# Scaling the softmax rows on GpSimd in place of VectorE, in an attention block between two LoRA mixture layers

## The chip, the cores and the metric

The program runs on one core of a Trainium2 chip. The metric is the time of one execution on the device, in microseconds (us). Lower is better. Its engines are named as the profile names them: PE is TensorE's matmul, PEld its weight load, DVE is VectorE, ACT is ScalarE, POOL is GpSimd, SP is SyncE, which issues most of the transfers.

## The reference

The input x has 4 sequences of 256 tokens with 512 features. It goes through three layers, each added to it: half a dense layer with 8 LoRA experts of which two are chosen for each token, an attention layer, and the first layer again. The attention is what the change touches:

```
q = (x @ wq)  32 heads of 128;  k, v = x @ wk, x @ wv  8 heads of 128
q, k = rope(q), rope(k)
scores = q k^T * 128**-0.5, allowed where j <= i and j > i - 128
attn = softmax(scores)
x = x + (attn @ v) @ wo
```

With sequences of 256 and a window of 128, a block of 128 queries has allowed keys only in its own block (at or before its diagonal) and in the block before it (past its diagonal).

## The kernel before

Every matmul of float32 data is done as three matmuls of rounded parts (hi\*hi, hi\*lo, lo\*hi). So each operand is split: ACT writes the rounded part `hi`, and DVE or POOL subtracts it from the source to get `lo`. DVE does it where the source is in PSUM, POOL where it is in SBUF.

The attention is a loop over 8 groups, one for each head of k and v. A group g has two halves (`hf` 0 and 1, two sequences each), and a half has 8 slots `s`: two sequences times four query heads. The unit of softmax work is numbered u = 16 g + 8 hf + s. The groups 1 to 6 are one loop body; groups 0 and 7 are written out apart. Each engine runs its own instruction stream in the fixed order of its own `group` function, and semaphores tie the streams together. In one slot:

- PE computes a ninth part of the projections of q, k and v for the next half (`project`, L1102, 9 matmuls), then the scores of unit u+1 (`scores`, L1121 to L1124), then the two transposes of the probabilities of unit u-1 (`p_transpose`, L1132). In slots 1 and 5 it goes on with probabilities times v for the sequence before (`values`, L1145), in slots 2, 3, 6 and 7 with the product with wo (`out_project`, L1160), which in slots 3 and 7 waits for the sum that DVE adds to x in the same slot (`x_add`, L841).
- DVE runs `softmax_norm` of unit u (the inverse of the row sums, L819, and two multiplications of prob, 128x128 each, L822), then `rope_sum` (L787) and `rope_cos` (L778), then the lower part of the transposed probabilities of u-1 (`p_lo`, L828), then `softmax_min` of unit u+1 (L806 to L814). Where a slot has them, `x_add` comes first and `o_lo` (L834) last.
- ACT computes the exponentials of unit u (`softmax_exp`, L550), splits weights, copies the half-swapped projection for rope (`rope_swap`, L523), and writes the upper part of the transposed probabilities of u-1 (`p_hi`, L558).
- POOL multiplies the swapped copy by the sines (`rope_sin`, L368), masks the transposed probabilities of u-1 (`p_part`, L375), computes the lower part of q or k (`rope_lo`, L385), and then the lower parts of the next weights (`weights`, L360). These stand at fixed slots: four of wo in slot 4 of half 0, one of wk in slot 5, two of wq in slot 7 and two in slot 0 of half 1, one of wv in slot 2 of half 1.

In half 1 of group 7 nothing more is projected. DVE's `ffn_start` begins the last layer there, and POOL runs `norm_rstd(2, ...)` in slots 1 and 5: 14 small dependent operations (L238 to L249) and a memset, between the slot's other work and its `p_part`.

The probabilities of a unit lie in `prob[:, s % 2, 0:2*P]`, those of the next unit in the other half of the buffer. The semaphore `norm_done` tells PE that a unit is scaled.

```
wait(pe, ptlo_done, u)        # in p_transpose(u, s), behind pe.wait_ge(norm_done, u + 1)
```

Of the kernel before, what the change touches and what calls it, by code (L numbers as in the profile page):

```python
# [24 lines left out]
P = 128  # L25
# [50 lines left out]
def macaron(nc, x_in, wq, wk, wv, wo, w_base, b_base, w_router, lora_a, lora_b, ident_in, mask_in, side_in, rope_in, out):  # L76
    ctx = ExitStack()
    with ctx:
        def sb(name, shape, dt=F32):
            return ctx.enter_context(nc.sbuf_tensor(name, shape, dt))  # L80

        def sem(name):
            return ctx.enter_context(nc.semaphore(name))
# [24 lines left out]
        prob = sb("prob", [P, 2, 3 * P])  # L108
# [8 lines left out]
        rinv = sb("rinv", [P, 2, 2])  # L117
# [73 lines left out]
        part_done = sem("part_scores_done")  # L191
        s_done, min_done, exp_done = sem("scores_done"), sem("min_done"), sem("exp_done")
        rinv_done, norm_done = sem("rinv_done"), sem("norm_done")
        parted, mask_turn = sem("pT_parted"), sem("mask_turn")
        t_done, pthi_done, ptlo_done = sem("pT_done"), sem("pT_hi"), sem("pT_lo")
        pv_done, othi_done, otlo_done = sem("pv_done"), sem("oT_hi"), sem("oT_lo")
        c_done, x_added = sem("wo_done"), sem("attn_x_done")
# [11 lines left out]
        def wk_pos(g):  # L209
            return 10 * g  # L210

        def wq_pos(g, i):
            return 10 * g + 1 + i

        def wv_pos(g):
            return 10 * g + 5

        def wo_pos(g, i):
            return 10 * g + 6 + i
# [106 lines left out]
        @block.gpsimd  # L326
        def _(pool):
            nc.gpsimd.memset(ones, 1.0).then_inc(preset, 1)
            nc.gpsimd.memset(ebuf[:, :, :, :], -1.0).then_inc(preset, 1)
            nc.gpsimd.memset(two[:, :, :], -1.0).then_inc(preset, 1)  # L330
            zero = nc.gpsimd.to_reg(0.0)

            def bias(f, t):

                if f == 0 and t == 0:
                    pool.wait_ge(prep_hi, 8)
                pool.wait_ge(xn_done, NT * 2 * f + t + 1)
                nc.gpsimd.tensor_tensor(x[:, t, :], x[:, t, :], half_bias[:, :], ALU.add).then_inc(biased, 1)

            steps = [0]  # L340

            def then(ins):

                steps[0] += 1
                ins.then_inc(pool_step, 1)
                pool.wait_ge(pool_step, steps[0])

            def norm_rstd(ln, t0, t1):

                pool.wait_ge(aggr, NT * ln + t1)  # L350
                rstd_steps(nc.gpsimd, then, t0, t1)
                nc.gpsimd.memset(gate_pool[:, :], 0.0).then_inc(rstd_done, 1)

            def split_lo(n, slot, hi, lo):

                pool.wait_ge(conv_hi, n + 1)
                src = raw[:, slot, :]
                if len(hi.shape) == 3:
                    src = src.rearrange("p (t n) -> p t n", t=KT)
                nc.gpsimd.tensor_tensor(lo, src, hi.bitcast(F32), ALU.subtract).then_inc(conv_lo, 1)  # L360

            def rope_sin(j, m):

                r = 5 * j + m
                w = swap[:, m % 2, :].rearrange("p (b s) -> p b s", b=2)
                tab = rope[:, 1 if m == 0 else 3, :].unsqueeze(1).broadcast_to([P, 2, SEQ])
                pool.wait_ge(swap_done, r + 1)
                nc.gpsimd.tensor_tensor(w, w, tab, ALU.mult).then_inc(t2_done, 1)  # L368

            def p_part(u, s):  # L370

                pool.wait_ge(ptlo_done, u + 1)
                pool.sem_inc(mask_turn, 1)
                h = s % G
                nc.gpsimd.affine_select(pT_both[:, :, 2, h, :], pT_both[:, :, 1, h, :].bitcast(F32),  # L375
                                        pattern=[[0, 2], [1, P]], compare_op=ALU.is_ge, fill=zero,
                                        base=0, channel_multiplier=-1).then_inc(parted, 1)

            def rope_lo(j, m, par):

                r = 5 * j + m
                hi = k[0][:, par, :] if m == 0 else q[0][:, par, m - 1, :]
                lo = k[1][:, par, :] if m == 0 else q[1][:, par, m - 1, :]
                pool.wait_ge(qhi_done, r + 1)
                nc.gpsimd.tensor_tensor(lo, rot[:, m % 2, :], hi.bitcast(F32), ALU.subtract).then_inc(qlo_done, 1)  # L385

            def weights(g, hf, s, last):
                if hf == 0 and s == 4:
                    for i in range(G):
                        split_lo(wo_pos(g, i), (6 + i) % RING, wo_s[0][:, i, :], wo_s[1][:, i, :])  # L390
                if hf == 0 and s == 5 and not last:
                    split_lo(wk_pos(g + 1), (6 + 4) % RING, wk_s[0][:, :, :], wk_s[1][:, :, :])
                if (hf, s) in ((0, 7), (1, 0)) and not last:
                    for i in ((0, 1) if hf == 0 else (2, 3)):
                        split_lo(wq_pos(g + 1, i), (6 + 5 + i) % RING, wq_s[0][:, i, :], wq_s[1][:, i, :])
                if hf == 1 and s == 2 and not last:
                    split_lo(wv_pos(g + 1), (6 + 9) % RING, wv_s[0][:, :, :], wv_s[1][:, :, :])

            def group(g, first, last):
                for hf in range(2):  # L400
                    for s in range(SLOTS):
                        split, m = (ENDS.get(c) if not (last and hf == 1) else None for c in (s - 1, s))
                        if m is not None and m < 5:
                            rope_sin(2 * g + hf + 1, m)
                        if last and hf == 1 and s in (1, 5):
                            norm_rstd(2, s // 2, s // 2 + 2)
                        if not (first and hf == 0 and s == 0):
                            p_part(16 * g + 8 * hf + s - 1, s - 1)
                        if split is not None and split < 5:
                            rope_lo(2 * g + hf + 1, split, 1 - hf)  # L410
                        weights(g, hf, s, last)

            for t in range(NT // 2):
                bias(0, t)
            norm_rstd(0, 4, NT)
            split_lo(0, 0, wk_s[0][:, :, :], wk_s[1][:, :, :])
            for i in range(KT):
                split_lo(1 + i, (1 + i) % RING, wq_s[0][:, i, :], wq_s[1][:, i, :])
            for t in range(NT // 2, NT):
                bias(0, t)  # L420
            norm_rstd(1, 0, 2)
            norm_rstd(1, 2, 4)
            split_lo(5, 0, wv_s[0][:, :, :], wv_s[1][:, :, :])
            for m in range(6):
                if m < 5:
                    rope_sin(0, m)
                if m:
                    rope_lo(0, m - 1, 0)
            group(0, True, False)
            with pool.Fori(1, KV - 1) as g:  # L430
                group(g, False, False)
            group(KV - 1, False, True)
            p_part(16 * KV - 1, SLOTS - 1)
            for t in range(NT):
                bias(1, t)
# [222 lines left out]
        def _(dve):  # L658
# [155 lines left out]
                nc.vector.tensor_reduce(prob[:, s % 2, 2 * P:3 * P], sm[:, s % 2, P:3 * P].rearrange("p (a n) -> p n a", a=2),  # L814
                                        axis=mybir.AxisListType.X, op=ALU.min).then_inc(min_done, 1)

            def softmax_norm(u, s):
                dve.wait_ge(exp_done, u + 1)
                nc.vector.reciprocal(rinv[:, s % 2, :], rsum[:, s % 2, :]).then_inc(rinv_done, 1)  # L819
                dve.wait_ge(rinv_done, u + 1)  # L820
                for i, (lo, hi) in enumerate(((0, P), (P, 2 * P))):
                    last = nc.vector.tensor_scalar(prob[:, s % 2, lo:hi], prob[:, s % 2, lo:hi],  # L822
                                                   rinv[:, s % 2, i:i + 1], None, ALU.mult)
                last.then_inc(norm_done, 1)

            def p_lo(u, s):
                dve.wait_ge(pthi_done, u + 1)
# [9 lines left out]
            def x_add(beta, b, i):  # L837

                dve.wait_ge(c_done, 2 * beta + i + 1)
                wait(dve, x_added, 2 * beta + i)  # L840
                nc.vector.tensor_tensor(x[:, 2 * b + i, :], C[:, :], x[:, 2 * b + i, :], ALU.add).then_inc(x_added, 1)  # L841
# [17 lines left out]
            def group(g, first, last):  # L859
                for hf in range(2):  # L860
                    for s in range(SLOTS):
                        u, beta, b = 16 * g + 8 * hf + s, 4 * g + 2 * hf + s // G, 2 * hf + s // G
# [5 lines left out]
                            x_add(beta - 1, (b - 1) % BATCH, 0)  # L868
                        if s % G == 0 and not (first and b < 2):
                            x_add(beta - 2, (b - 2) % BATCH, 1)  # L870
                        softmax_norm(u, s)
                        if split is not None and split < 5:
                            rope_sum(2 * g + hf + 1, split)
                        if m is not None and m < 5:
# [90 lines left out]
            v_diff(0)  # L965
            softmax_min(0, 0)
            group(0, True, False)
            with dve.Fori(1, KV - 1) as g:
                group(g, False, False)
            group(KV - 1, False, True)  # L970
            x_add(4 * KV - 2, BATCH - 2, 1)
            p_lo(16 * KV - 1, SLOTS - 1)
# [330 lines left out]
```

## Time and profile before

| what | value |
|---|---|
| time, median of 3 runs (lowest to highest) | 747.13 us (746.68 to 747.5) |
| time of the profiled execution | 746.33 us |
| its span, first to last instruction | 744.6 us |
| mean granted clock of TensorE | 0.998 |
| PE busy | 717.2 us (96%) |
| DVE busy | 601.0 us (81%) |
| ACT busy | 413.3 us (56%) |
| POOL busy | 396.5 us (53%) |

The span is the stretch that the profile shows; 1.7 us of the profiled execution lie outside it. Busy shares are means over the whole span. In the table of groups of instructions, L822 is DVE's scaling: 256 instructions, 83.3 us, 367 ns each in the mean. The period of one group is 77.6 us.

### The profile page before, as it was taken

The numbers are of one execution on the slowest core, as the hardware profiler recorded it, in microseconds if no ns is written. First come the engines' busy times: TensorE is split into PE (matmuls) and PEld (weight loads), VectorE is DVE, ScalarE is ACT, GpSimd is POOL, SyncE is SP. The second block draws the span as 40 slices with busy tenths as digits, with TensorE's granted clock in tenths as the row PEclk, the third lists the DMA queues.
The fourth block names the chain that finished last, engine by engine and source line by source line (L and its number), as shares of the span: only waits on it lengthen the run. The fifth ranks groups of instructions, "written<-read, shape, count | busy, mean of one in ns | idle before, by whom it ended". The sixth has DMA issues, their size and how long they took to land.

```text
span 744.6 us, 13949 instructions
## 1 busy us (share of the span) xinstructions
PE 717.2 (96%) x3692; PEld 603.1 (81%) x3692; DVE 601.0 (81%) x2060; ACT 413.3 (56%) x1122; POOL 396.5 (53%) x466
## 2 busy tenths in 40 slices
PE   8899789999999999999999999999999999998998
PEld 5787667888888888888888888888888888887786
DVE  6898778877887888878887888788878887788795
ACT  3324475657655676556655766576656665754320
POOL 0674268634864477438653765367535863462420
PEclk9999999999999999999999999999999999999999
DMA  8240003100220022002200120013000310030002
GB/s 266 73 158 16 0 3 98 43 1 2 73 70 1 0 70 70 0 0 70 56 14 0 56 70 14 0 32 94 15 0 0 99 28 1 1 114 1 0 31 85
DMA packets 25843, 32.13 MB, mean 43 GB/s; under 512 B 5833, under 2 KB 14281, under 8 KB 25298
## 3 DMA queue, kind: packets, MB, share of 16 engines
q1 hardware_dynamic: 25232, 30.69, 13.1%
q10 hardware_dynamic: 578, 1.05, 0.4%
q8 instruction: 14, 0.23, 0.1%
q14 instruction: 19, 0.16, 0.1%
HBM read 27.54 MB, written 4.19 MB: 43 GB/s over the span
## 4 chain that ended last, share of the span: by engine, by line
PE 70%; DVE 20%; issue 5%; ACT 3%; DMA 1%; POOL 1%; DVEq 0%; SPq 0%; ACTq 0%
PE bank L1102 26%; PE bank L1160 19%; PE bank L1145 6%; PE bank L1124 5%; PE bank L1068 5%; PE bank L1132 3%; DVE prob L822 2%; DVE rot L787 2%; DVE oT_lo L834 2%; DVE prob L814 1%; DVE sm L807 1%; PE bank L1121 1%; DVE rot L778 1%; ACT prob L550 1%; DVE pT_hi_lo L828 1%
## 5 line engine op out<-in xcount | busy, mean ns | idle before, releaser
L368 POOL TENSOR_TENSOR swap<-swap,rope 128x512 f32<-128x512 f32 x80 | 110.1, 1377 | 129.8 <-ACT swap L523 129.8
L550 ACT ACTIVATE prob<-sm,nmax 128x128 f32<-128x128 f32 x128 | 51.5, 403 | 151.4 <-DVE prob L814 150.4
L375 POOL TENSOR_SCALAR_AFFINE_SELECT pT_hi_lo<-pT_hi_lo 128x256 fp32r<-128x256 f32 x128 | 52.3, 409 | 140.3 <-DVE pT_hi_lo L828 139.8
L523 ACT ACTIVATE swap<-bank 64x512 f32<-64x512 f32 x160 | 94.9, 593 | 10.6 <-PE bank L1102 6.7
L558 ACT ACTIVATE pT_hi_lo<-bank 128x256 fp32r<-128x256 f32 x128 | 48.9, 382 | 71.5 <-PE bank L1132 50.6
L822 DVE TENSOR_SCALAR prob<-prob,rinv 128x128 f32<-128x128 f32 x256 | 83.3, 367 | 4.5
L385 POOL TENSOR_TENSOR q_lo<-rot,q_hi 128x512 fp32r<-128x512 f32 x64 | 82.6, 1291 | 6.9 <-ACT q_hi L531 6.9
L1160 PE MATMUL bank<-wo_hi,oT_hi 128*128 128x512 f32 x256 | 74.6, 413 | 5.0 <-DVE x L841 5.0
L828 DVE TENSOR_TENSOR pT_hi_lo<-bank,pT_hi_lo 128x256 fp32r<-128x256 f32 x128 | 53.6, 418 | 29.4 <-ACT pT_hi_lo L558 29.2
L1102 PE MATMUL bank<-xnT_hi,wq_hi 128*128 128x512 f32 x256 | 71.4, 391 | 2.2 <-DVE v_lo L798 1.4
L1102 PE MATMUL bank<-xnT_lo,wq_hi 128*128 128x512 f32 x256 | 73.4, 389 | 0.0
L1102 PE MATMUL bank<-xnT_hi,wq_lo 128*128 128x512 f32 x256 | 72.3, 395 | 0.0
L1160 PE MATMUL bank<-wo_hi,oT_lo 128*128 128x512 f32 x256 | 68.6, 390 | 0.0
L1160 PE MATMUL bank<-wo_lo,oT_hi 128*128 128x512 f32 x256 | 68.5, 389 | 0.0
L787 DVE TENSOR_TENSOR rot<-rot,swap 128x512 f32<-128x512 f32 x80 | 64.5, 807 | 0.0
L778 DVE TENSOR_TENSOR rot<-bank,rope 128x512 f32<-128x512 f32 x80 | 54.8, 685 | 9.4 <-ACT swap L523 9.0
L1145 PE MATMUL bank<-pT_hi_lo,v_hi 128*128 128x512 f32 x192 | 62.1, 404 | 0.0
L1102 PEld LDWEIGHTS bank<-xnT_hi,wq_hi 128*128 128x128 f32 x256 | 47.8, 188 | 13.2 <-DVE v_lo L798 1.8
L1124 PE MATMUL bank<-k_hi_lo,q_hi 128*128 128x256 f32 x256 | 57.7, 308 | 0.0
L819 DVE RECIPROCAL rinv<-rsum 128x2 f32<-128x2 f32 x128 | 20.6, 161 | 45.9 <-ACT prob L550 45.9
L1160 PEld LDWEIGHTS bank<-wo_lo,oT_hi 128*128 128x128 f32 x256 | 48.0, 188 | 10.4
L1160 PEld LDWEIGHTS bank<-wo_hi,oT_lo 128*128 128x128 f32 x256 | 48.1, 188 | 10.1
(150 smaller groups left out, 1768.9 us busy)
## 6 DMA issues: line engine op xcount, KB each, us to landing
raw<-in_L_attn_wq SPq DMA_DIRECT2D x32, 256.0 KB, 3.0
raw<-in_L_attn_wo SPq DMA_DIRECT2D x32, 256.0 KB, 2.6
x<-in_L_attn_x SPq DMA_DIRECT2D x4, 512.0 KB, 7.3
raw<-in_L_attn_wk SPq DMA_DIRECT2D x8, 256.0 KB, 2.7
raw<-in_L_attn_wv SPq DMA_DIRECT2D x8, 256.0 KB, 2.6
out<-x SPq DMA_DIRECT2D x8, 256.0 KB, 2.0
raw<-in_L_ffn_W_base ACTq DMA_DIRECT2D x4, 256.0 KB, 5.1
wb_keep_hi<-q_hi SPq DMA_DIRECT2D x1, 1024.0 KB, 4.9
```

What stands on the lines that cost most here:

```text
L368: nc.gpsimd.tensor_tensor(w, w, tab, ALU.mult).then_inc(t2_done, 1)
L385: nc.gpsimd.tensor_tensor(lo, rot[:, m % 2, :], hi.bitcast(F32), ALU.subtract).then_inc(qlo_done, 1)
L523: last = nc.scalar.activation(swap[a:a + half, m % 2, :], A[m % 2][b:b + half, :], ACT.Copy)
L550: last = nc.scalar.activation(prob[:, s % 2, lo:hi], src, ACT.Exp, bias=nmax[:, s % 2, i:i + 1], scale=-1.0, accum_out=rsum[:, s % 2, i:i ...
L778: nc.vector.tensor_tensor(rot[:, m % 2, :].rearrange("p (b s) -> p b s", b=2), A[m % 2][:, :].rearrange("p (b s) -> p b s", b=2), rope[:, ...
L787: nc.vector.tensor_tensor(rot[:, m % 2, :], rot[:, m % 2, :], swap[:, m % 2, :], ALU.add).then_inc(sum_done, 1)
L822: last = nc.vector.tensor_scalar(prob[:, s % 2, lo:hi], prob[:, s % 2, lo:hi], rinv[:, s % 2, i:i + 1], None, ALU.mult)
L828: nc.vector.tensor_tensor(pT[1][:, 0:2, s % G, :], T[:, 0:2 * P].rearrange("p (c n) -> p c n", c=2), pT[0][:, 0:2, s % G, :].bitcast(F32), ...
L1102: last = mm(A[m % 2][:, :], w, xnT[b][:, d, hf * HALF:(hf + 1) * HALF], start=(i == 0), stop=(i == 11))
L1124: last = mm(S[s % 2][:, 2 * P:4 * P], q[a][:, hf, h, q1], k[c][:, hf, b * SEQ:(b + 1) * SEQ], start=(n == 0), stop=(n == 2))
L1145: last = mm(O[i][:, :], v[a][:, par, 2 * b + kb, :], pT[c][:, blk, :, :], start=(n == 0), stop=(n == len(todo) - 1))
L1160: last = mm(C[:, :], oT[a][:, par, i, h, :], wo_s[c][:, h, :], start=(h == 0 and n == 0), stop=(h == G - 1 and n == 2))
```

## The change

The two multiplications leave DVE's `softmax_norm`, which keeps the inverse and is called `softmax_recip`. POOL gets a `softmax_norm` of its own, which waits for the inverse (`rinv_done`), raises a new semaphore `scale_turn` that nothing waits for, and does the same two multiplications on the same buffers. It stands first in POOL's slot, ahead of `rope_sin`, `p_part`, `rope_lo` and `weights`. DVE no longer waits for its own inverse. DVE's next `softmax_min`, which writes the last third of the other half of `prob`, can now run while POOL scales.

```
+            def softmax_norm(u, s):            # on gpsimd
+
+                pool.wait_ge(rinv_done, u + 1)
+                pool.sem_inc(scale_turn, 1)
+                for i, (lo, hi) in enumerate(((0, P), (P, 2 * P))):
+                    last = nc.gpsimd.tensor_scalar(prob[:, s % 2, lo:hi], prob[:, s % 2, lo:hi],
+                                                   rinv[:, s % 2, i:i + 1], None, ALU.mult)
+                last.then_inc(norm_done, 1)
...
                     for s in range(SLOTS):     # group(), on gpsimd
                         split, m = (ENDS.get(c) if not (last and hf == 1) else None for c in (s - 1, s))
+                        softmax_norm(16 * g + 8 * hf + s, s)
                         if m is not None and m < 5:
                             rope_sin(2 * g + hf + 1, m)
...
-            def softmax_norm(u, s):            # on vector
+            def softmax_recip(u, s):
                 dve.wait_ge(exp_done, u + 1)
                 nc.vector.reciprocal(rinv[:, s % 2, :], rsum[:, s % 2, :]).then_inc(rinv_done, 1)
-                dve.wait_ge(rinv_done, u + 1)
-                for i, (lo, hi) in enumerate(((0, P), (P, 2 * P))):
-                    last = nc.vector.tensor_scalar(prob[:, s % 2, lo:hi], prob[:, s % 2, lo:hi],
-                                                   rinv[:, s % 2, i:i + 1], None, ALU.mult)
-                last.then_inc(norm_done, 1)
```

## Rows read from the trace of the kernel before

**Rows 1.** The page: busy time, share and instructions of each engine.

```profile
PE 717.2 (96%) x3692; PEld 603.1 (81%) x3692; DVE 601.0 (81%) x2060; ACT 413.3 (56%) x1122; POOL 396.5 (53%) x466
```

**Rows 2.** Busy time of each engine in one period of the loop.

```profile
343.29:420.87 77.58, 76.91 (x398) 65.50 (x397) 62.62 (x217) 48.40 (x133) 44.98 (x47) 1.00 0.11 34
```

**Rows 3.** The chain that ended last, 334 to 362 us: start, us, what.

```profile
343.29 1.33 DVE prob L822
...
353.35 3.01 PE bank L1160 x12
```

**Rows 4.** What PE waited for, 85 to 700 us: total us, times, longest.

```profile
PE bank L1160 <- DVE x L841: 4.8, 7, 0.7
PE bank L1132 <- DVE pT_hi_lo L828: 4.5, 5, 1.3
```

**Rows 5.** Timeline of PE in group 3: start, us, instruction, [idle before].

```profile
346.72 0.38 PE L1132 MATMUL bank<-ident,prob 128*128 128x128 f32 x2
...
353.35 1.17 PE L1160 MATMUL bank<-wo_hi,oT_hi 128*128 128x512 f32 x4 [0.67 <-DVE x L841]
```

**Rows 6.** Timeline of POOL in the same stretch.

```profile
342.00 5.04 POOL L360 TENSOR_TENSOR wo_lo<-raw,wo_hi 128x512 fp32r<-128x512 f32 x4
347.00 1.29 POOL L368 TENSOR_TENSOR swap<-swap,rope 128x512 f32<-128x512 f32 x1
348.25 0.40 POOL L375 TENSOR_SCALAR_AFFINE_SELECT pT_hi_lo<-pT_hi_lo 128x256 fp32r<-128x256 f32 x1
348.63 1.28 POOL L360 TENSOR_TENSOR wk_lo<-raw,wk_hi 128x512 fp32r<-128x512 f32 x1
349.87 1.75 POOL L368 TENSOR_TENSOR swap<-swap,rope 128x512 f32<-128x512 f32 x1
```

**Rows 7.** Timeline of DVE in the same stretch.

```profile
342.37 0.17 DVE L819 RECIPROCAL rinv<-rsum 128x2 f32<-128x2 f32 x1 [0.95 <-ACT prob L550]
342.57 2.04 DVE L822 TENSOR_SCALAR prob<-prob,rinv 128x128 f32<-128x128 f32 x2
...
348.66 1.80 DVE L787 TENSOR_TENSOR rot<-rot,swap 128x512 f32<-128x512 f32 x1
...
352.52 0.68 DVE L841 TENSOR_TENSOR x<-bank,x 128x512 f32<-128x512 f32 x1
```

**Rows 8.** Groups of instructions on POOL: shapes, count, busy us, mean ns, idle before.

```profile
L385 POOL TENSOR_TENSOR q_lo<-rot,q_hi 128x512 fp32r<-128x512 f32 x64 | 82.6, 1291 | 6.9 <-ACT q_hi L531 6.9
L375 POOL TENSOR_SCALAR_AFFINE_SELECT pT_hi_lo<-pT_hi_lo 128x256 fp32r<-128x256 f32 x128 | 52.3, 409 | 140.3 <-DVE pT_hi_lo L828 139.8
...
L248 POOL TENSOR_SCALAR nt<-nt 128x2 f32<-128x2 f32 x12 | 2.3, 192 | 1.1
```

**Rows 9.** Timeline of half 1 of group 7 on PE.

```profile
676.09 0.38 PE L1132 MATMUL bank<-ident,prob 128*128 128x128 f32 x2
677.42 1.11 PE L1041 MATMUL bank<-ident,swap 128*128 128x128 f32 x8 [0.95 <-DVE swap L690]
...
681.90 1.16 PE L1068 MATMUL bank<-q_hi,xnT_hi 128*128 128x512 f32 x4 [0.34 <-DVE xnT_lo L697]
```

**Rows 10.** Timeline of the same half on POOL.

```profile
671.54 0.21 POOL L238 TENSOR_SCALAR var<-mv 128x2 f32<-128x2 f32 x1 [2.94 <-DVE mv L676]
...
675.48 0.10 POOL L352 MEMSET gate_pool<- 128x1 f32 x1
675.60 0.77 POOL L375 TENSOR_SCALAR_AFFINE_SELECT pT_hi_lo<-pT_hi_lo 128x256 fp32r<-128x256 f32 x2
```

**Rows 11.** Timeline of the same half on DVE.

```profile
671.37 0.13 DVE L819 RECIPROCAL rinv<-rsum 128x2 f32<-128x2 f32 x1
671.53 0.48 DVE L822 TENSOR_SCALAR prob<-prob,rinv 128x128 f32<-128x128 f32 x2
```

**Rows 12.** Timeline of PE in half 0 of group 0.

```profile
112.54 0.98 PE L1102 MATMUL bank<-xnT_hi,wv_hi 128*128 128x512 f32 x3 [1.07 <-DVE rot L778]
...
113.94 0.38 PE L1132 MATMUL bank<-ident,prob 128*128 128x128 f32 x2
```

**Rows 13.** Timeline of POOL, group 0.

```profile
109.27 5.02 POOL L360 TENSOR_TENSOR wo_lo<-raw,wo_hi 128x512 fp32r<-128x512 f32 x4
```

More of the change, by code:

```diff
@@ L193, in macaron @@
         rinv_done, norm_done = sem("rinv_done"), sem("norm_done")
-        parted, mask_turn = sem("pT_parted"), sem("mask_turn")
+        parted, mask_turn, scale_turn = sem("pT_parted"), sem("mask_turn"), sem("scale_turn")
         t_done, pthi_done, ptlo_done = sem("pT_done"), sem("pT_hi"), sem("pT_lo")
@@ L870, in group @@
                             x_add(beta - 2, (b - 2) % BATCH, 1)
-                        softmax_norm(u, s)
+                        softmax_recip(u, s)
                         if split is not None and split < 5:
```

## The prediction, made before the change was run

> **What bounds the kernel now.** I read the page's busy times first: PE is busy 96% of the span, DVE 81%, POOL 53% [rows 1]. So a change off PE pays only where PE waits, and there is little of that. The busy times of one period of the loop say the same more sharply: in 77.58 us PE is busy for 76.91, POOL for 44.98 [rows 2]. Then PE's waits: in the whole attention PE stands at the product with wo for DVE's `x_add` seven times, about 0.68 us each (4.8 us in total), once in each of groups 0 to 6, and five times at the transposes for `p_lo`, 4.5 us in all, which are in group 0 and in half 1 of group 7 [rows 4]. The chain that ended last shows where the seven come from: in half 0 it leaves PE for DVE and returns at 353.35, and its longest single step there is one scaling of 1.33 us that ends 344.6 [rows 3]. The timelines of the three engines around it explain that step. POOL starts four lower parts of wo at 342.00 and is done at 347.04 [rows 6]; DVE's two scalings begin at 342.57 and take 2.04 us for the pair, against 0.48 where no long POOL operation runs [rows 7, 11]. Two POOL operations end at 342.00 + 2 x 1.26 = 344.52, and that is where the pair ends: each scaling waited until an operation of POOL was over. POOL wasn't slowed by it (5.04 / 4 = 1.26 each).
>
> **What is removed.** DVE loses 256 scalings, 83.3 us busy at 367 ns. Most of that lies beside a busy PE. On the path that PE waits for, slot 5 loses the whole 2.04 us. DVE's `rope_cos`, which could begin at 344.54, can now begin when ACT's swapped copy is there, about 343.6.
>
> **What is added.** POOL gets 256 multiplications with one tensor input, 128x128. It has none of that size. The nearest rows are the mask, one input, 128x256, 409 ns, and the small ones, 128x2, 192 ns [rows 8]. They give (409 - 192) / 254 = 0.85 ns an element, so 192 + 126 x 0.85 = 300 ns for one. Rows on POOL follow one another with some 0.04 us of overlap (347.00 + 1.29 to 348.25 [rows 6]), so the pair takes D = 0.56. The scalar that it fetches for each partition may cost more: the bound from above is the rate of two-input work, (1291 - 192) / 510 = 2.15 ns an element [rows 8], which is 463 ns each and D = 0.9. From below it can't be under two fixed costs and some data, D = 0.4. I take D = 0.6, by the one-input rows with a little for the scalar.
>
> The Trainium skill, "GPSIMD Engine Reference", section 3.1, gives about 1.8 cycles an element as the best loop of one input; at its 1.2 GHz that would make D about 0.73 by estimate, and the sum below some 1.1 us larger. Its section 4.1 says that one-input work runs roughly at line rate; the mask row is on that side (0.85 ns an element), and I go by the row.
>
> POOL's load rises by 16 x 0.6 = 9.6 us a period, to 54.6 of 77.6: it doesn't become the bound. What counts is when it gets to each unit. A unit is scaled in slot s and transposed by PE late in slot s+1, so there is slack of a slot. I went through the sixteen units of a period with POOL's rows. In fifteen POOL is ready well before PE: even behind the weights of wq the margin is over 1 us. There the scaling is hidden, and `rope_sin` behind it has its sums a slot later.
>
> **The unit that is not hidden** is the one of slot 5, half 0. POOL's slot 4 ends with the four lower parts of wo, so its scaling can't start before 347.00. It ends at 347.6, PE can take it some 0.12 later (the same step as from `x_add`'s end, 353.20, to PE at 353.35 [rows 5, 7]): the transposes begin at 347.82 instead of 346.72 [rows 5]. PE is late by 1.10.
>
> Then the old wait pays back. PE would now come to the product with wo of slot 7 at 353.35 - 0.67 + 1.10 = 353.78. Is DVE's `x_add` over by then? `rope_sum` waits for POOL's sines, which are late by D: 347.6 + 1.29 = 348.9. Before, `rope_sum` came at 348.66, just behind the start of the wk part, and stood to the end of it, 1.80 in place of 0.69 [rows 6, 7]. Now it comes at about 349.1, while the mask runs, and gets its turn when the mask ends at 349.3. It ends at 350.0, before: 350.46. So DVE is some 0.4 earlier, `x_add` ends at 352.8, and PE doesn't wait. A group of the loop costs 1.10 - 0.67 = 0.43 us; six of them (1 to 6) make 2.6.
>
> **Group 0.** Without the scaling DVE's chain at the start is about 0.4 shorter once; after that ACT's cycle (exponentials, swapped copy, upper part) is as long as DVE's and keeps the rest. PE's wait of 1.07 for `rope_cos` goes [rows 12]. But POOL's four parts, 109.27 to 114.25 [rows 13], move up only by that 0.4, so PE transposes at 113.85 + 0.6 + 0.12 = 114.6 instead of 113.94 [rows 12]. The lateness of 0.65 meets this group's own wait of 0.68 at `x_add`: about 0.
>
> **Group 7.** Slot 5 of half 0 is late by 1.10 as well, and there is no wait at `x_add` to take it up (seven, not eight [rows 4]). In half 1 a second queue matters: POOL's slot 1 now has the scaling, then `norm_rstd`, 4.04 us (671.54 to 675.58 [rows 10]), the mask, and then the scaling of slot 2. Before, DVE was through with its inverse at 671.5 [rows 11]. Shifted by 1.1: inverse 672.6, scaling to 673.4, `norm_rstd` to 677.45, mask to 677.85, second scaling to 678.45, PE at 678.57 instead of 676.09 [rows 9]. PE waited after it until 677.42 for the normalized x, so what follows, 678.57 + 0.15, is late by 1.3; the next wait, 0.34 at 681.90, takes up its size: +1.0 for the group, its 1.10 included. After that PE has no wait on the softmax, and the second `norm_rstd`, in slot 5, leaves its next scaling 0.7 us of margin.
>
> **The sum:** 2.6 + 0 + 1.0 = +3.6 us. Against the profiled execution that is 746.33 + 3.6 = 749.9; the median of the runs lies 0.8 above it, so I give 747.13 + 3.6 = 750.7 us, 0.5% slower. Each 0.1 in D is worth 0.1 in seven or eight groups and once more in group 7, about 0.85 us.
>
> **The rivals.** (a) POOL's scaling is as slow as two-input work, D = 0.9: +0.3 x 8.5 = 2.6 more, 753.3. The one-input row of the mask speaks against it, and the scalar for each partition, which no row shows on POOL at this size, for it. (b) `rope_sum` loses its turn to the wk part once more: DVE is then 1.2 later, `x_add` ends at 354.05 and PE starts at 354.2, +0.85 a group in place of 0.43: seven times 0.4, 753.6. DVE got its turn between two POOL operations at 343.3 and 344.5, which speaks against it. The Trainium skill, "SBUF — State Buffer", section "Who interferes with whom", says that of a GpSimd instruction and a VectorE one with two SBUF inputs the one that starts first keeps the shared pair for the whole instruction; the 1.80 us of `rope_sum` agree, and by that rule too the order of arrival decides. (c) No measurable change (within 0.2%, 1.5 us, which is about what runs of this kernel can tell apart): D near 0.4 and a gain of 0.5 at the start, +0.2 x 6 + 0.8 - 0.5 = +1.5, 748.6. (d) The other side, faster: DVE's lost 2.04 us in slot 5 is the whole story, and PE doesn't stand at the transposes, because POOL's parts of wo are over earlier than the rows say, or start earlier with DVE out of the way. Then seven waits of 0.68 and about 1 us at the start go: -5.5, 741.6. It decides if POOL is free by 345.9 in place of 347.04. Against it: nothing that POOL waits for before 342.00 is moved by the change, and its four operations weren't held up.
>
> **Numbers.** The forecast with D between 0.45 and 0.75, 749.4 to 752.0: 0.48. (a) or worse 0.17, (b) 0.15, (c) 0.13, (d) 0.07. The range from 748.2 to 755.0 leaves out (d), half of (c) and a slow tail. Slower by over 0.2%: 0.80; within: 0.13; faster: 0.07.
>
> **What the profile after should show.** POOL has 256 rows of 128x128 at about 0.3 us. In each group one wait of PE at L1132 for POOL, 1.0 to 1.1 us, right behind the four parts of wo; the waits at L1160 for `x_add` are gone; a period is 78.0 in place of 77.58. One wait of some 2.5 us or less at L1132 stands in half 1 of group 7, behind `norm_rstd`. DVE's busy share falls from 81% to some 68%. The prediction is wrong if PE's transposes of slot 6 don't wait for POOL, if the scaling takes over 0.45 us, or if PE still waits for `x_add` in slot 7.

## The result: 1.2% slower, more than twice the loss forecast

The changed kernel takes 756.27 us in the median of four runs (754.49 to 758.34), the one before 746.90 (746.62 to 747.5) beside it. The ratio is 1.0125, with a 95% interval from 1.0111 to 1.0139: +9.4 us, where +3.6 was forecast, and above the range. The profiled execution took 754.49 us, its span is 752.8, against 744.6 before: +8.2.

The page of the changed kernel, its busy times (they answer to [rows 1]) and the group of the scalings:

```profile
PE 717.9 (95%) x3692; PEld 603.2 (80%) x3692; DVE 524.0 (70%) x1804; ACT 411.3 (55%) x1122; POOL 565.2 (75%) x722
...
L375 POOL TENSOR_SCALAR prob<-prob,rinv 128x128 f32<-128x128 f32 x256 | 167.0, 663 | 88.8 <-DVE rinv L829 88.0
```

DVE is 77 us less busy, and POOL 169 more: the same 256 multiplications that took DVE 367 ns each take POOL 663 in the mean. PE has the same 3692 matmuls and is busy for 0.7 us more; the rest of the 8.2 us is time in which PE waits. What PE waited for, 85 to 720 us (to be laid beside [rows 4], which end at 700; us in total, times, longest; the lines have shifted: L1137 is the transposes, L1165 the product with wo):

```profile
PE bank L1137 <- POOL prob L375: 17.8, 13, 2.4
PE bank L1137 <- DVE pT_hi_lo L833: 1.8, 2, 1.3
...
PE bank L1165 <- DVE x L846: 0.3, 1, 0.3
```

The seven waits for `x_add` are gone (the one left lies at 715.8, in the last layer), and thirteen for the new scaling stand in their place. Eight of those are the unit of slot 5, one in each group: 2.36 us in group 0, 1.38 to 1.41 in the others. Timelines of group 3 of the changed kernel, POOL, PE and DVE (they answer to [rows 5 to 7]):

```profile
343.93 5.07 POOL L360 TENSOR_TENSOR wo_lo<-raw,wo_hi 128x512 fp32r<-128x512 f32 x4
348.97 1.18 POOL L375 TENSOR_SCALAR prob<-prob,rinv 128x128 f32<-128x128 f32 x2
350.12 1.28 POOL L368 TENSOR_TENSOR swap<-swap,rope 128x512 f32<-128x512 f32 x1
351.35 0.41 POOL L384 TENSOR_SCALAR_AFFINE_SELECT pT_hi_lo<-pT_hi_lo 128x256 fp32r<-128x256 f32 x1
351.72 1.73 POOL L360 TENSOR_TENSOR wk_lo<-raw,wk_hi 128x512 fp32r<-128x512 f32 x1
```

```profile
348.52 0.28 PE L1129 MATMUL bank<-k_hi_lo,q_lo 128*128 128x256 f32 x1
350.20 0.44 PE L1137 MATMUL bank<-ident,prob 128*128 128x128 f32 x2 [1.41 <-POOL prob L375]
350.53 1.17 PE L1165 MATMUL bank<-wo_hi,oT_hi 128*128 128x512 f32 x4
...
355.88 0.28 PE L1129 MATMUL bank<-k_hi_lo,q_lo 128*128 128x256 f32 x1
356.00 0.38 PE L1137 MATMUL bank<-ident,prob 128*128 128x128 f32 x2
356.13 1.18 PE L1165 MATMUL bank<-wo_hi,oT_hi 128*128 128x512 f32 x4
```

```profile
351.52 0.78 DVE L797 TENSOR_TENSOR rot<-rot,swap 128x512 f32<-128x512 f32 x1 [1.98 <-POOL swap L368]
...
354.36 0.68 DVE L846 TENSOR_TENSOR x<-bank,x 128x512 f32<-128x512 f32 x1
```

The order is the one forecast: four parts of wo, the scaling right behind them, PE at the transposes 0.05 us after it. The pair takes 1.18 us in place of 0.6. `x_add` is over at 355.04, 1.1 before PE wants it at 356.13. PE's own rows show a second thing. In slot 7, where nothing is awaited, the product with wo starts 0.25 behind the last scores (355.88 to 356.13). In slot 6, which transposes the unit of slot 5, it starts 2.01 behind (348.52 to 350.53). So the wait that the view calls 1.41 costs 1.76: what follows a wait starts later than the idle time alone says, by some 0.3.

That is why I count by half periods, from one set of `v_transpose` (four transposes of `swap`, once a half) to the next. Where PE waits for nothing, in most halves 1 of both kernels, a half takes 38.3 us.

| stretch | before | after | difference |
|---|---|---|---|
| span start to the first set | 86.47 | 86.64 | +0.2 |
| group 0, half 0 | 36.97 | 37.11 | +0.1 |
| half 0 of groups 1 to 6 | 39.25 to 39.27 each | 40.02 to 40.14 each | +4.9 in all |
| half 1 of groups 0 to 6 | 38.31 or 38.33 each | 38.31 to 38.42 each | +0.1 in all |
| group 7, half 0 | 38.37 | 39.96 | +1.6 |
| last set to the end of the span | 79.01 | 80.24 | +1.2 |

These make up the 8.2, but for rounding. The last line holds half 1 of group 7, where PE waits again for POOL:

```profile
674.97 0.41 PE L1137 MATMUL bank<-ident,prob 128*128 128x128 f32 x2 [0.44 <-POOL prob L375]
679.75 0.44 PE L1137 MATMUL bank<-ident,prob 128*128 128x128 f32 x2 [1.71 <-POOL prob L375]
685.78 0.44 PE L1137 MATMUL bank<-ident,prob 128*128 128x128 f32 x2 [2.26 <-POOL prob L375]
```

The rest of the 9.4, some 1.2 us, lies between the executions: the profiled one is the fastest of its four. Its mean granted clock was 0.998, and the others, at 755.9, 756.64 and 758.34 us, had 0.995, 0.998 and 0.991. The second of them had the same clock and took 2.1 us longer, so the clock alone doesn't explain the difference.

### The profile page after: what moved, and what is told of

Its sections match the earlier page's. It is cut to its first block, busy times and chain, and to the rows that moved or that the text cites. A ratio compares the mean times of both kernels' runs of the same rounds, so it can differ in the third digit from the quotient of the medians.

```text
span 752.8 us, 14077 instructions
## 1 busy us (share of the span) xinstructions
PE 717.9 (95%) x3692; PEld 603.2 (80%) x3692; DVE 524.0 (70%) x1804; ACT 411.3 (55%) x1122; POOL 565.2 (75%) x722
## 4 chain that ended last, share of the span: by engine, by line
PE 74%; DVE 9%; POOL 8%; issue 5%; ACT 2%; DMA 1%; POOLq 0%; SPq 0%; DVEq 0%
PE bank L1107 28%; PE bank L1165 22%; PE bank L1150 6%; PE bank L1129 6%; PE bank L1137 4%; POOL wo_lo L360 3%; PE bank L1073 3%; POOL prob L375 2%; PE bank L1126 2%; DVE stats L685 1%; PE bank L1090 1%; DVE swap L700 1%; PE bank L1116 1%; PE bank L1127 1%; POOL q_lo L394 1%
## 5 line engine op out<-in xcount | busy, mean ns | idle before, releaser
L375 POOL TENSOR_SCALAR prob<-prob,rinv 128x128 f32<-128x128 f32 x256 | 167.0, 663 | 88.8 <-DVE rinv L829 88.0
L368 POOL TENSOR_TENSOR swap<-swap,rope 128x512 f32<-128x512 f32 x80 | 103.5, 1293 | 10.0 <-ACT swap L533 10.0
L394 POOL TENSOR_TENSOR q_lo<-rot,q_hi 128x512 fp32r<-128x512 f32 x64 | 88.8, 1387 | 6.9 <-ACT q_hi L541 6.9
L1165 PE MATMUL bank<-wo_hi,oT_hi 128*128 128x512 f32 x256 | 74.6, 413 | 0.3 <-DVE x L846 0.3
L1165 PE MATMUL bank<-wo_lo,oT_hi 128*128 128x512 f32 x256 | 68.6, 390 | 0.0
L1165 PE MATMUL bank<-wo_hi,oT_lo 128*128 128x512 f32 x256 | 68.6, 390 | 0.0
L1137 PE MATMUL bank<-ident,prob 128*128 128x128 f32 x256 | 49.7, 276 | 19.6 <-POOL prob L375 17.8
L1165 PEld LDWEIGHTS bank<-wo_lo,oT_hi 128*128 128x128 f32 x256 | 48.0, 188 | 10.5
L1165 PEld LDWEIGHTS bank<-wo_hi,oT_lo 128*128 128x128 f32 x256 | 48.1, 188 | 10.1
```

Source lines behind the costliest of these rows:

```text
L375: last = nc.gpsimd.tensor_scalar(prob[:, s % 2, lo:hi], prob[:, s % 2, lo:hi], rinv[:, s % 2, i:i + 1], None, ALU.mult)
L1137: last = tp(T[:, c * P:(c + 1) * P], prob[:, s % 2, c * P:(c + 1) * P], ident[:, :])
L1165: last = mm(C[:, :], oT[a][:, par, i, h, :], wo_s[c][:, h, :], start=(h == 0 and n == 0), stop=(h == G - 1 and n == 2))
```

## The experiments

Three questions: is the size of the pair the error, is the unit of slot 5 really the whole cost, and what limits the kernel once both are mended. Each ratio below is to the kernel before, run beside it.

### The price of one scaling, alone

The changed kernel, with 17 extra GpSimd instructions behind its last output, of sizes from 128x32 to 128x512: a multiplication by a scalar for each partition, by a constant, and a two-input one whose second input is that scalar, broadcast.

> The changed kernel with 17 extra GpSimd instructions after its last work, each waiting for the one before: multiplication of 128 x n by a scalar of each partition read from SBUF (n = 32, 64, 128, 256, 512), the same by a constant, the same as a two-input multiplication with the scalar broadcast, and one 128x256 with two broadcast scalars. Theory pointer (fetching the scalar of each partition is what the forecast left out): by a constant 128x128 takes 0.30 us and with the scalar 0.60, a constant difference of 0.3 at every n. Rival rate (the multiplication itself is slow): by a constant it also takes 0.58 to 0.60 and both grow by over 2 ns an element. Two inputs, broadcast: 0.19 + n x 2.15 ns, so 0.46 at 128 and 0.74 for the 128x256.

It took 766.32 us with them. Their groups on POOL, in the stretch where nothing else runs (busy us, mean ns):

```profile
L453 POOL TENSOR_SCALAR swap<-swap,rinv 128x512 f32<-128x512 f32 x1 | 1.6, 1562 | 0.1
L457 POOL TENSOR_SCALAR swap<-swap 128x512 f32<-128x512 f32 x1 | 1.5, 1487 | 0.1
L461 POOL TENSOR_TENSOR swap<-swap,rinv 128x512 f32<-128x512 f32 x1 | 1.0, 1038 | 0.1
...
L461 POOL TENSOR_TENSOR swap<-swap,rinv 128x256 f32<-128x256 f32 x1 | 0.6, 612 | 0.1
...
L453 POOL TENSOR_SCALAR swap<-swap,rinv 128x128 f32<-128x128 f32 x1 | 0.6, 602 | 0.1
...
L457 POOL TENSOR_SCALAR swap<-swap 128x128 f32<-128x128 f32 x1 | 0.5, 527 | 0.1
...
L461 POOL TENSOR_TENSOR swap<-swap,rinv 128x128 f32<-128x128 f32 x1 | 0.4, 398 | 0.1
```

This is one execution, with one instruction of each size. From 128x128 to 128x512 the scaling grows by 960 ns for 384 elements: 2.5 ns an element. The constant saves 75 ns at either size and no rate. The two-input form with the broadcast scalar has (1038 - 398) / 384 = 1.67 ns an element. So the one-input multiplication is the slowest of the three, slower by the element than even the subtraction of two tensors in [rows 8] (1291 ns for 512). The Trainium skill, "GPSIMD Engine Reference", section 4.1, calls one-input work on GpSimd roughly line rate. The trace disagrees for this instruction, which at 2.5 ns an element is slower than the two-input form at 1.67, and the measurement decides.

### The same scaling, made shorter in two ways

e1_constant leaves the normalization out: it multiplies by 1.0 and keeps all waits.

```
# e1_constant
-                   rinv[:, s % 2, i:i + 1], None, ALU.mult)
+                   1.0, None, ALU.mult)
# e2_one_broadcast: one instruction for both halves of the unit
+                w = prob[:, s % 2, 0:2 * P].rearrange("p (a n) -> p a n", a=2)
+                nc.gpsimd.tensor_tensor(w, w, rinv[:, s % 2, :].unsqueeze(2).broadcast_to([P, 2, P]),
+                                        ALU.mult).then_inc(norm_done, 1)
```

> The changed kernel with GpSimd's two multiplications by the constant 1.0 in place of the inverse of the row sums, so the probabilities are not normalized; all waits stay. Theory pointer: 0.30 us each, the pair 0.56, and the time falls to about 751 us (the forecast's sum with its own D); the wait of PE at the transposes of slot 6 falls from 1.41 to about 0.8. Rival rate: nothing moves, 756, pair 1.18.

> The two multiplications on GpSimd become one two-input multiplication, 128x256, with the two inverses broadcast. By the two-input rate of the kernel before (192 ns and 2.15 ns an element) it takes 0.74 us in place of 1.18 for the pair, so PE's wait in each group falls by 0.44, and the time by 0.44 x 8.5 = 3.7 us, to 752.5. If the broadcast operand is as dear as the scalar, it takes 1.0 or more and the time stays over 755.

| kernel | scaling of a unit, group 3 | PE's wait, group 3 | half 0 | median of runs | ratio |
|---|---|---|---|---|---|
| changed | 1.18 | 1.41 | 40.08 | 756.27 | 1.0125 [1.0111, 1.0139] |
| e1_constant | 1.04 | 1.23 | 39.89 | 754.06 | 1.0096 [1.0079, 1.0113] |
| e2_one_broadcast | 0.64 | 0.82 | 39.48 | 749.40 | 1.0027 [1.0017, 1.0038] |

(The second column is POOL's row of the unit of slot 5 in group 3.) The constant takes 0.14 off the pair, so the rate and not the scalar makes it dear, as in e0. e2 was expected at 752.5 and came 3 us lower: its scaling was 0.1 shorter than the two-input rows gave, and each 0.1 was worth more than 0.85. PE's wait follows the length of the scaling nearly one to one: -0.54 in the scaling gives -0.59 in the wait and -0.60 in the half. The loss falls from 9.4 to 2.3 us with nothing else touched. With the pair at the length that was forecast, the kernel loses 0.3%, and the recorded 750.7 would have been 1.3 too high.

The trace of e2_one_broadcast shows a cost that can follow a long wait. PE in group 0, and three stretches around that wait (the number after the last engine is the granted clock):

```profile
115.16 0.52 PE L1136 MATMUL bank<-ident,prob 128*128 128x128 f32 x2 [1.76 <-POOL prob L375]
115.35 2.04 PE L1164 MATMUL bank<-wo_hi,oT_hi 128*128 128x512 f32 x4
117.19 1.83 PE L1164 MATMUL bank<-wo_lo,oT_hi 128*128 128x512 f32 x4
118.85 1.07 PE L1164 MATMUL bank<-wo_hi,oT_lo 128*128 128x512 f32 x4
```

```profile
113.40:115.16 1.76, 0.00 (x2) 0.00 (x1) 1.22 (x3) 1.72 (x6) 1.76 (x3) 1.00 0.64 179
115.30:118.60 3.30, 3.30 (x10) 2.62 (x10) 2.23 (x5) 1.20 (x3) 3.30 (x4) 0.51 0.36 112
119.00:122.00 3.00, 3.00 (x17) 2.50 (x15) 2.43 (x6) 1.92 (x7) 3.00 (x4) 1.00 0.30 87
```

Behind 1.76 us without a matmul the clock stands at 0.51 of full, the 1.2 GHz level, for 3.3 us, in which four matmuls take 2.04 in place of 1.17 us. That costs by estimate 3.3 x 0.49 = 1.6 us once. The same was in the profiled executions of e0_probe behind a wait of 2.26, of e1_constant behind one of 2.13, and of e3_wo_moved (below) behind one of 2.27. It was not there in the changed kernel, behind waits of 2.36 and 2.26, nor in e1_constant behind one of 2.18. So such a wait brings the lower level in some executions and not in others, and no run here shows what decides. The changed kernel's other executions may have had it; that is not shown, since only the fastest of them was profiled.

### Only the unit of slot 5 goes back to VectorE

```
-                        softmax_norm(16 * g + 8 * hf + s, s)      # on gpsimd
+                        if not (hf == 0 and s == 5):
+                            softmax_norm(16 * g + 8 * hf + s, s)
...
                         softmax_recip(u, s)                       # on vector
+                        if hf == 0 and s == 5:
+                            scale_here(u, s)       # the two multiplications of the kernel before
```

> VectorE scales the one unit of each group whose scaling stands behind the four parts of wo on GpSimd (slot 5 of half 0), GpSimd the other fifteen. Theory (only this unit is not hidden in the loop): PE's waits at the transposes for GpSimd go in all eight groups, the wait at x_add of up to 0.68 comes back in seven, a period is 77.6 again, and what is left over the kernel before is half 1 of group 7, 1 to 3 us: 748 to 750. Rival (GpSimd's fuller queue delays PE in many slots, or the shared port does): the period stays over 78.0 and the time over 752.

Measured: 744.40 us (743.5 to 745.24, seven runs), ratio 0.9968 [0.9956, 0.9979]. One unit in sixteen turns a loss of 9.4 us into a gain of 2.7, and the kernel is now faster than before. In the profiled execution half 0 takes 38.4 us in the loop, and half 1 takes 38.7: PE is no longer held up in half 0, so it comes to the first unit of half 1 just as POOL is done with it. That scaling stands behind the first two wq parts and ends at 359.18, and PE's transposes start at 359.23, 0.25 behind the last scores in place of 0.12. I had expected 748 to 750, with the waits for `x_add` back, since DVE's pair is as long as ever. They did not come. DVE in group 3:

```profile
340.44 2.04 DVE L836 TENSOR_SCALAR prob<-prob,rinv 128x128 f32<-128x128 f32 x2
...
346.30 0.78 DVE L798 TENSOR_TENSOR rot<-rot,swap 128x512 f32<-128x512 f32 x1 [0.40 <-POOL swap L368]
...
349.15 0.68 DVE L855 TENSOR_TENSOR x<-bank,x 128x512 f32<-128x512 f32 x1
```

The pair still stands to the end of two POOL operations (four take 5.07 us from 339.87, so the second ends at about 342.4, and the pair at 342.48). What is gone is the second delay of [rows 7], the 1.80 us of `rope_sum`, because slot 6 has no scaling on DVE ahead of it: it comes at 346.30, before the wk part starts at 346.48. So the waits for `x_add` before the change were the sum of two delays on DVE, and here taking the second away ends them.

### The parts of wo are moved out of the way

Two of the four lower parts of wo right behind the scaling of slot 4, two behind that of slot 5, in the changed kernel (e3), in the kernel before (e4, at the same places, with no scaling there), and with the broadcast scaling (v1).

```
-                if hf == 0 and s == 4:
-                    for i in range(G):
+            def wo_part(g, hf, s):
+                if hf == 0 and s in (4, 5):
+                    for i in ((0, 1) if s == 4 else (2, 3)):
                         split_lo(wo_pos(g, i), (6 + i) % RING, wo_s[0][:, i, :], wo_s[1][:, i, :])
...
                         softmax_norm(16 * g + 8 * hf + s, s)      # not in the kernel before
+                        wo_part(g, hf, s)
```

> The changed kernel with GpSimd's four parts of wo placed otherwise: two right behind the scaling in slot 4, two right behind the scaling in slot 5 (half 0), so the scaling of slot 5 stands in front of the last two. The scaling is as slow as before, 1.18 us a pair. Theory (place decides: only what stands in front of this one unit): scaling of slot 5 ends at 344.3 on the time scale of the kernel before, PE takes it at 346.6 with no wait, and the wait for x_add goes too: half 0 of a group takes 38.6 in place of 40.1 us, 743 us in all. Rival (a slow scaling on a full GpSimd queue costs anyway): the period stays over 77.6 and the time over 747.

> The kernel before, with scaling on VectorE, and GpSimd's parts of wo placed the same way (two first in slot 4, two first in slot 5). If the gain of the other run is only the earlier rope_sin and wk parts, this one has it as well: the wait for x_add goes, 742 to 743 us. If it is VectorE's freedom from the scaling (the pair still waits for GpSimd's wo parts, 2.0 us), the seven waits stay and the time is 746 to 747.

> The changed kernel with one broadcast multiplication for the pair (0.61 us in place of 1.18) and the parts of wo moved. If place decides, the cheaper scaling only helps where GpSimd is still late: group 7's last half, 0.5 to 1 us under the run with the parts moved alone, so 742 to 742.5. If cost decides in the loop as well, 2 us or more under it.

| kernel | median (range, runs) | ratio |
|---|---|---|
| e3_wo_moved | 749.76 (748.84 to 751.52, 6) | 1.0035 [1.0022, 1.0048] |
| e4_before_wo_moved | 742.18 (740.74 to 744.22, 4) | 0.9929 [0.9907, 0.9950] |
| v1_bcast_wo | 741.67 (740.57 to 742.53, 4) | 0.9923 [0.9904, 0.9943] |

The first is a miss by 7 us. PE no longer stands at the transposes in slot 6, but at `x_add` in slot 7, in group 0 (1.28) and in groups 2 to 6 (0.81 or 0.82 each). POOL, DVE and PE of e3_wo_moved in group 3:

```profile
348.51 1.31 POOL L368 TENSOR_TENSOR swap<-swap,rope 128x512 f32<-128x512 f32 x1
349.76 0.42 POOL L384 TENSOR_SCALAR_AFFINE_SELECT pT_hi_lo<-pT_hi_lo 128x256 fp32r<-128x256 f32 x1
350.13 1.30 POOL L360 TENSOR_TENSOR wk_lo<-raw,wk_hi 128x512 fp32r<-128x512 f32 x1
```

```profile
349.94 2.09 DVE L800 TENSOR_TENSOR rot<-rot,swap 128x512 f32<-128x512 f32 x1 [0.89 <-POOL swap L368]
```

```profile
354.92 1.16 PE L1168 MATMUL bank<-wo_hi,oT_hi 128*128 128x512 f32 x4 [0.82 <-DVE x L849]
```

`rope_sum` comes 0.18 us after the mask has begun, and stands for 2.09 us: past the end of the mask at 350.18, to the end of the wk part at 351.43. In the changed kernel it came 0.17 us after the mask had begun, and took 0.78. It got its turn when the mask ended: it is over 0.54 us after the end of the mask (351.76 to 352.30), as the held one of [rows 7] is over 0.55 after the end of the wk part (349.91 to 350.46), and it is the next POOL operation that grew, the wk part, to 1.73. The order of arrival is the same and the outcome is not. In group 1 of e3_wo_moved itself it came 0.17 us after the mask had begun (194.96) and took 0.78, and PE had no wait there. No row tells why. In v1_bcast_wo, in the two groups of the loop with a wait at `x_add` (1.35), DVE's row in group 1 is longer still:

```profile
191.52 3.62 DVE L799 TENSOR_TENSOR rot<-rot,swap 128x512 f32<-128x512 f32 x1
```

POOL runs the wk part, the scaling and `rope_sin` back to back in it (191.47 to 194.58), and DVE passes two boundaries between them without its turn. This is rival (b)'s mechanism, at a place where the forecast's rule was that DVE gets its turn at the next boundary. The Trainium skill, "SBUF — State Buffer", section "Who interferes with whom", says that whichever of the two starts first keeps the shared pair until its instruction is over; the traces agree as far as one instruction goes, and show that a row of GpSimd's can keep it over three.

The medians of the other two are close to what was expected (742 to 743 for e4 if the order of wo is the gain, 742 to 742.5 for v1). But v1 is 8 us under e3 where 0.5 to 1 was expected: with the parts of wo moved, the price of the scaling still decides in the loop.

e4_before_wo_moved is the other half of the answer: the kernel before gains 4.3 us by the order of wo alone. The parts of wo cost either kernel; the change made them cost more.

### The last half on VectorE

```
+                        if not (last and hf == 1):                # on gpsimd
+                            softmax_norm(16 * g + 8 * hf + s, s)
...
+                        if last and hf == 1:                      # on vector
+                            scale_here(u, s)
```

> The changed kernel with VectorE scaling the eight units of half 1 of group 7, where GpSimd has 14 small operations in front of a scaling. The profiles put +1.3 us on that half (80.27 against 79.01 from its first transposes to the end). Theory: they go, 1.3 us less, about 755.0 by the median, and PE's waits of 1.7 and 2.3 for the scaling are gone from it. Rival (that half is bound by VectorE and gives nothing back): same as the changed kernel.

Measured: 754.32 us (753.14 to 755.45), ratio 1.0098 [1.0075, 1.0121]. The interval overlaps that of the changed kernel, so the runs alone do not tell the two apart. The traces do: from the last set of `v_transpose` to the end it is 78.9 us against 80.24, and in half 1 of group 7 PE waits for `p_lo` again (0.44 and 1.27) in place of the 1.71 and 2.26 for POOL. The queue there is worth about 1.4 us.

### Both mended, and the part of wk as well

The wk part of slot 5 moves to the end of slot 6, where neither `rope_sum` nor the scaling meets it. With the broadcast scaling (v3), in the kernel before (e7), and in the changed kernel with its pair of 1.18 us (e8).

```
-                if hf == 0 and s == 5 and not last:
+                if hf == 0 and s == 6 and not last:
                     split_lo(wk_pos(g + 1), (6 + 4) % RING, wk_s[0][:, :, :], wk_s[1][:, :, :])
```

> The version with the broadcast scaling and the parts of wo moved, and the part of wk moved from the end of slot 5 to the end of slot 6, so that GpSimd has nothing to start while rope_sum of slot 6 waits for the shared port. In the run without this, rope_sum was held for 3.6 us in two of six groups of the loop. Theory (rope_sum loses its turn at the boundary of back-to-back GpSimd operations): no wait for x_add in any group, both halves take 38.3 us, 740.5 to 741. Rival (it is held by the other operations just as well): the two long halves come back, 741.7.

> The kernel before, scaling on VectorE, with the parts of wo and of wk placed as in that version. If the placing is all of the gain it is as fast as the version with the scaling on GpSimd, within 1 us: 741 to 742. If freeing VectorE is worth something of its own, it stays 2 us or more above.

> The changed kernel, with its slow scaling (1.18 us a pair), and wo and wk placed as in that version. If the price of the scaling only counts where it is late, it costs 0.5 to 1.5 us over the broadcast version, in group 7: 741.5 to 742.5, and the wait of 0.82 for x_add that the run with only wo moved had in each group is gone. If the fuller GpSimd queue costs by itself, the loop stays above 77.0 a period, 745 or more.

| kernel | median (range, runs) | ratio | half 0 in the loop | half 1 in the loop |
|---|---|---|---|---|
| v3_bcast_wo_wk | 738.47 (738.06 to 739.03, 4) | 0.9890 [0.9875, 0.9905] | 38.33 | 38.33 |
| e7_before_wo_wk | 743.49 (742.9 to 744.77, 5) | 0.9961 [0.9948, 0.9975] | 38.33 or 38.98 | 38.31 or 38.33 |
| e8_wo_wk_slow | 746.99 (745.22 to 748.14, 10) | 1.0005 [0.9996, 1.0015] | 38.33 | 38.84 |

v3_bcast_wo_wk is the fastest kernel of the study, 8.2 us under the one before, and 2 us under what was expected. Two halves of its loop, 340 to 416.66, by engine (PE, PEld, DVE, ACT, POOL):

```profile
340.00:416.66 76.66, 76.66 (x398) 65.50 (x397) 53.39 (x184) 48.04 (x132) 56.80 (x63) 1.00 0.12 34
```

PE is busy in all of it: in the loop there is nothing left to gain but matmuls. The same order without the change is 5.0 us behind, and the best order tried for the kernel before (e4) is 2.9 behind by the ratios, so moving the scaling to GpSimd is a gain once its price and place are right. Of the 4.5 us between the profiled executions of e7 and v3, 2.0 lie in three halves 0 of the loop, 1.5 in half 0 of group 0, 0.5 behind the last set, and 0.7 ahead of the attention, where the two kernels are alike and e7 ran from 36 to 41 us at a granted clock of 0.66, v3 at 1.00. The cause of the 2.0 shows in DVE of e7_before_wo_wk:

```profile
341.75 2.71 DVE L825 TENSOR_SCALAR prob<-prob,rinv 128x128 f32<-128x128 f32 x2
344.38 0.68 DVE L781 TENSOR_TENSOR rot<-bank,rope 128x512 f32<-128x512 f32 x1
```

DVE's pair stands 2.71 us beside the two moved parts of wo. `rope_cos` comes behind it, and in group 3 PE waits for that (0.33).

e8_wo_wk_slow was expected at 741.5 to 742.5, so that is a miss too. In the loop the long waits of slots 6 and 7 are gone and half 0 is at 38.33, but half 1 is 0.5 longer than the matmuls, in every group of the loop. The rival of the expectation holds: the fuller queue costs by itself, with a period of 77.2. POOL and PE of e8_wo_wk_slow at the change of halves:

```profile
356.95 2.54 POOL L360 TENSOR_TENSOR wq_lo<-raw,wq_hi 128x512 fp32r<-128x512 f32 x2
359.48 1.18 POOL L375 TENSOR_SCALAR prob<-prob,rinv 128x128 f32<-128x128 f32 x2
```

```profile
360.40 0.28 PE L1132 MATMUL bank<-k_hi_lo,q_lo 128*128 128x256 f32 x1
360.71 0.44 PE L1140 MATMUL bank<-ident,prob 128*128 128x128 f32 x2
```

POOL has no gap from 351.2 on, wk now lies ahead of the wq parts, and the scaling ends at 360.66, just before PE starts at 360.71 instead of 360.52. It is the same failure at another unit, that of slot 0 of half 1, and the one that e5 has there: with the long pair POOL has no slack to take up a weight that is moved. In v3_bcast_wo_wk the scaling at this place takes 0.61 and POOL idles ahead of it. Of the 7.1 us between the profiled executions of e8 and v3 the loop holds 3.1. The rest lies in group 0 (2.0) and in the last half of group 7 (2.2), where the queue of e6 is unchanged: waits of 0.99, 1.39 and 2.25.

## Why the prediction was wrong, step by step

- **What bounds the kernel, and the unit that isn't hidden:** right. The transposes of the unit of slot 5 wait behind the four parts of wo in every group, and e5 shows that this one unit is worth the whole loss in the loop and more. That the other fifteen are ready with "over 1 us" to spare holds only while PE is late: in e5, with the long pair and PE on time, the unit behind the wq parts has nothing left. The order of POOL's operations, the end of the waits for `x_add` and the place of the second loss, half 1 of group 7, were as written.
- **The term that failed is D,** "I take D = 0.6, by the one-input rows with a little for the scalar". It is 1.18, that is 0.6 us for each scaling, and "the scaling takes over 0.45 us" was one of the prediction's own signs of being wrong. By its own sum D = 1.18 gives 3.6 + 5.8 x 0.85 = +8.5, against the 8.2 between the profiled executions, so this one term carries the miss. The interval given for it, 0.4 to 0.9, didn't hold it either, since its upper end took two-input work as the dearest kind. The mask, a select, has one input but is another operation, and its 0.85 ns an element says nothing of a multiplication's 2.5. Rival (a) had the right direction and gave the scalar for each partition as its reason; e0 shows that the scalar is 75 of the 602 ns, and that the multiplication itself is the rest; e1 bears it out in the kernel. With e2's 0.64 us the kernel lands at 749.4, inside the range. In part that is luck: at D = 0.64 the sum would say +3.9, where +2.3 was measured, because most of the errors that follow lean the other way.
- **A wait was priced at its idle time.** "A group of the loop costs 1.10 - 0.67 = 0.43": the `x_add` wait of 0.67 lengthened its half by 39.26 - 38.33 = 0.93, and a wait of 0.82 (e2) costs 1.15. At a pair of 0.64 the two leave 1.15 - 0.93 = 0.22 in place of 0.43. With D = 1.18 it is 40.08 - 38.33 = 1.75, less 0.93: 0.82, and 4.9 for the six groups.
- **A slip in the sum:** 347.6 + 0.12 is 347.72 and not 347.82. By its own terms PE is late by 1.00, a group costs 0.33, and the forecast would be about +2.9, which is further off.
- **`rope_sum` "gets its turn when the mask ends":** right in the changed kernel, where it was over 0.54 us after the mask and `x_add` isn't late. It is no rule, though: in e3 and v1 it was passed over at such a boundary. Rival (b) was not what happened here, but it is what undid e3.
- **Group 0, about 0:** +0.1, but not by the recorded numbers. PE transposes at 115.14 in place of the forecast 114.6, and counted from the first set it is late by 1.03. That the half is longer by only 0.14 fits an `x_add` wait that had cost 0.9, as in the loop, and not its idle time of 0.68; the two errors cancel. The stretch ahead of it took +0.2.
- **Group 7, +1.0:** 2.8 (1.6 in half 0, 1.2 in half 1, which e6 gets back). In half 0 there is no wait to pay back, so the pair's 1.18 counts in full. The margin of 0.7 claimed behind the second `norm_rstd` was not there: the scaling behind it, of the unit of slot 6, came late again (0.30 at 702.94).
- **The sensitivity, 0.85 us for 0.1 in D:** too low. From e2 to the changed kernel the scaling grows by 0.54 us, and the stretch from the first set to the end of the span by 5.0 (661.2 to 666.1), in which e2's dip of the clock hides 1.6 by estimate: 6.6 us, or 1.2 for 0.1. Most of it is plain: in groups 1 to 7 half 0 lengthens by about 0.60 for the 0.54, which is 4.2, and the queue behind the last set adds 1.8.
- **What stays open:** the 1.2 us by which the median loss exceeds that between the profiled executions, and what decides whether DVE gets its turn between two GpSimd operations.

## What to carry to other kernels

An operation that moves to another engine is priced by the same operation there; if the trace has none, a neighbour with the same number of inputs is not a bound, and the range has to say so. A helper engine with 47% idle time is no shelter if it works in order: ask for each unit what stands ahead of it, and move the long, early-ready work (here the weights) behind the short work that the bounding engine waits for. Try the cheap forms too: one broadcast multiplication for both blocks turned the same move from a loss of 9.4 us into one of 2.3, and with the weights in better slots into a gain of 8.2.

## What the hardware showed that was not expected

- GpSimd's multiplication of one tensor by a scalar is slower than its multiplication of two tensors: 2.5 against 1.67 ns an element (128x512: 1562 and 1038 ns).
- A DVE operation with two SBUF inputs waited through three GpSimd operations in a row, 3.62 us in place of 0.69 (v1_bcast_wo, group 1). At nearly equal arrival, 0.17 or 0.18 us behind the start of one operation, it got its turn at the next boundary in the changed kernel and was passed over in e3_wo_moved.
- After a single wait of 1.8 to 2.3 us TensorE ran 3.3 us at the 1.2 GHz level in four of the profiled executions (granted clock 0.50 or 0.51); behind like waits in the changed kernel (2.36 and 2.26) it did not.
